# A two-attention, two-mixture kernel: norms and routing of five batches moved to other steps, exponentials cut into other pieces, causal copies of 384 and 320 columns

## The reference, cut to what matters

```
x = x + attn_a(layernorm(x))   # 16 heads of 64, relative bias, softmax over all 256 keys
x = x + ffn(layernorm(x))      # 8 experts, one per row (argmax of a router), gated
x = x + attn_b(layernorm(x))   # keys and values through a 128-wide latent, CAUSAL softmax
x = x + ffn(layernorm(x))      # the same experts again
```

```
scores = q @ k.T * scale (+ bias, or -inf above the diagonal)
attn   = softmax(scores, axis=-1)
out    = attn @ v ; heads joined ; @ w_out
```

## Time and profile before

| | |
|---|---|
| median of three runs | 674.76 us |
| lowest, highest | 671.71, 675.14 us |
| the profiled execution | 671.86 us |
| its span, first to last instruction | 670.6 us |
| TensorE busy | 637.2 us, 95% |
| ScalarE busy | 543.8 us, 81% |
| VectorE busy | 512.4 us, 76% |
| GpSimd busy | 354.6 us, 53% |

### The profile page before, as it was taken

How to read it: one execution, slowest core, us unless ns; L and a number is a source line. 1 busy time by engine, 2 the same in 40 slices (tenths; PEclk the granted TensorE clock), 3 DMA queues, 4 the chain that set the end, 5 groups by cost and what they waited for, 6 DMA issues and landing times. The chain is left out here.

```text
span 670.6 us, 22111 instructions
## 1 busy us (share of the span) xinstructions
PE 637.2 (95%) x7454; PEld 536.2 (80%) x7454; DVE 512.4 (76%) x2211; ACT 543.8 (81%) x1776; POOL 354.6 (53%) x669
## 2 busy tenths in 40 slices
PE   5899999999999999989999999999999999999997
PEld 5578787777778787879996788878788878878987
DVE  4977878987887878988656767787878777888833
ACT  3898888889898979775765999898989898986664
POOL 4454545566445744732116545464757574572746
PEclk9999999999999999999999999999999999999999
DMA  8999989999980000035521000000000000013140
GB/s 270 276 312 304 277 212 326 305 306 304 284 258 10 26 2 2 34 97 140 148 67 40 22 3 1 3 2 11 17 14 10 14 26 2 3 34 96 55 131 17
DMA packets 90319, 74.78 MB, mean 112 GB/s; under 512 B 12225, under 2 KB 87111, under 8 KB 90080
## 3 DMA queue, kind: packets, MB, share of 16 engines
q1 hardware_dynamic: 86512, 66.24, 35.0%
q0 software_dynamic: 2848, 6.33, 2.9%
q10 hardware_dynamic: 848, 0.79, 0.4%
HBM read 19.93 MB, written 54.00 MB: 110 GB/s over the span
## 5 line engine op out<-in xcount | busy, mean ns | idle before, releaser
L392 POOL TENSOR_SCALAR ring<-ring,rs 128x256 f32<-128x256 f32 (+1 forms) x500 | 218.3, 455 | 205.2 <-DVE rs L1310 204.8
L990 ACT ACTIVATE ring<-ring,mn 128x256 f32<-128x256 f32 (+1 forms) x512 | 242.0, 479 | 2.9 <-DVE mn L1298 2.8
L531 PE MATMUL ps<-ident,ring 128*128 128x128 f32 x896 | 124.9, 275 | 4.0 <-DVE ol L1270 2.9
L644 PE MATMUL ps<-qk 64*64 64x256 f32 (+1 forms) x2048 | 112.4, 356 | 1.4 <-DVE mn L1298 0.7
L531 PEld LDWEIGHTS ps<-ident,ring 128*128 128x128 f32 x896 | 101.6, 143 | 14.8 <-issue 7.3
L687 PE MATMUL ps<-pt,v 64*64 64x256 f32 (+3 forms) x2048 | 103.1, 339 | 6.4 <-ACT pt L977 5.6
L687 PEld LDWEIGHTS ps<-pt,v 64*64 64x64 f32 x2048 | 73.8, 133 | 37.6 <-ACT pt L977 18.6
L990 ACT ACTIVATION_READ_ACCUMULATOR ring<-ring,mn 128x1 f32 x512 | 99.9, 195 | 0.0
L1325 DVE COPY pt<-ps 128x512 f32<-128x512 f32 (+1 forms) x128 | 71.3, 557 | 32.7 <-PE ps L531 31.3
L962 ACT COPY qk<-ps 128x512 f32<-128x512 f32 x128 | 74.4, 581 | 21.3 <-PE ps L528 20.3
L644 PEld LDWEIGHTS ps<-qk 64*64 64x64 f32 x2048 | 65.8, 132 | 29.9 <-issue 12.4
(11 more groups left out here) (209 smaller groups left out, 1300.2 us busy)
## 6 DMA issues: line engine op xcount, KB each, us to landing
xs_scratch<-f_ys SPq DMA_DIRECT2D x16, 2064.0 KB, 22.0
yr_scratch<-f_ys SPq DMA_DIRECT2D x8, 1024.0 KB, 10.1
f_xs<-xs_scratch SPq DMA_DIRECT2D x50, 129.0 KB, 2.5
w<-in_W SPq DMA_DIRECT2D x16, 256.0 KB, 5.9
xs_scratch<-f_ys SPq DMA_DIRECT2D x2, 1677.0 KB, 20.9
yr_scratch<-f_ys SPq DMA_DIRECT2D x25, 64.0 KB, 1.8
T<-in_bias SPq DMA_DIRECT2D x2, 512.0 KB, 7.8
T<-in_bias SPq DMA_DIRECT2D x1, 1024.0 KB, 10.3
```

Of the source, the lines that this page charges most:

```text
L392: i = pool.tensor_scalar(part, part, rs[:, q], 1.0, ALU.mult, ALU.mult)
L531: return pe.transpose(out, src, ident[:, :])
L644: i = pe.matmul(PS[u % 2][hh][cols, 256 * it:256 * it + w], qk[rows, 128 * it + 64 * half_:128 * it + 64 * half_ + 64], qk[rows, 256:256 + ...
L990: i = act.activation(part, part, ACT.Exp, bias=mn[:, q], scale=-1.0, accum_out=sm[:, q])
```

## The change

Five things change, in the tables of lags and in the functions that read them.

1. For batches 0 to 4 (`CALM` = 5) the norms after the attention, the choice and the places move to other steps, given by `CALM_POST`, and VectorE does them in a new function `calm(s)`, called in even steps directly behind its copy of transposes `TR(s-4)`. Before, they stood before that copy, behind it in odd steps, or at the end of an odd step. The places are cut into two parts, two steps apart. TensorE's, ScalarE's and GpSimd's shares follow.
2. For batches 2 to 7 the norm before the attention moves one step earlier (`CALM_PRE`) and also into `calm(s)`.
3. The exponentials of an even unit are taken as piece (0,0) at the start of the next even step but before the copy `T(s)`, pieces (0,1) and (1,0) after the copy of transposes, and piece (1,1) in the odd step. Before, it was two pieces in the even step and two in the odd.
4. In the causal attention the transposes are spread over the two banks as 3 and 3 in place of 4 and 2. ScalarE copies 384 columns in place of 512, VectorE 320 columns in one run in place of 2 x 128.
5. The fetches of the last four x tiles in stage 1 (`FETCH`) move from steps 35, 39, 41, 43 to 18, 26, 32, 34.

The diff, cut to its core:

```diff
-POST = {"a": 14, "b": 15, "c": 16, "lg": 16, "gate": 17, "d": 18, "place": 18}
+POST = {"sums": 13, "pow": 13, "a": 14, "xn": 14, "b": 15, "c": 16, "lg": 16, "choose": 16, "gate": 17, "d": 18, "place": 18}
+CALM = 5
+CALM_POST = {"sums": 14, "pow": 14, "a": 20, "xn": 20, "b": 22, "c": 23, "lg": 23, "choose": 26, "gate": 27, "d": 28, "counted": 28, "place": 30}
+CALM_PRE = {"a": -8, "pow": -8, "a2": -6}
...
-FETCH = dict(zip((35, 39, 41, 43), range(*CH[1])))
+FETCH = dict(zip((18, 26, 32, 34), range(*CH[1])))
...
+    def keys_at(q, causal):
+
+        return ((0, 0), (1, 0), (1, 128), (0, 128))[q] if causal else (q // 2, 256 * (q % 2))
...
-            act.copy(pt[:, 0, :], PP[0][:, :]).then_inc(a_pt0, 1)
+            w = 384 if causal else 512
+            act.copy(pt[:, 0, 0:w], PP[0][:, 0:w]).then_inc(a_pt0, 1)
...
+            if s % 2 == 0 and 2 <= s < NU:
+                expo(s - 2, ALL[0])
             if 0 <= s < NU:
                 T(s)
...
-                expo(s - 3, (1,))
+                expo(s - 3, *ALL[3:])
...
-                expo(s - 2, (0, 1) if s % 2 or s == NU else (0,))
+                expo(s - 2, *(ALL if s % 2 or s == NU else ALL[1:3]))
...
-            late = slice(128 if causal else 0, 256)
-            dve.tensor_copy(*(a.rearrange("p (q i) -> p q i", q=2)[:, :, late] for a in (pt[:, 1, :], PP[1][:, :]))
-                            ).then_inc(v_pt1, 1)
+            r = slice(64, 384) if causal else slice(0, 512)
+            dve.tensor_copy(pt[:, 1, r], PP[1][:, r]).then_inc(v_pt1, 1)
...
+            calm(s)
             if s < NU and (b := post_at(s, "a")) is not None:
                 post_a2(b)
...
+        def calm(s):
+            if (b := calm_pre(s, "a")) is not None:
+                pre_a(b)
+            if (b := calm_pre(s, "a2")) is not None:
+                pre_a2(b)
+            if (b := calm_post(s, "sums")) is not None:
+                sums(b)
+            if (b := calm_post(s, "a")) is not None:
+                post_a(b)
+                post_a2(b)
+            if (b := calm_post(s, "choose")) in ROUTED:
+                decide(b)
+            if (b := calm_post(s, "counted")) in ROUTED:
+                place(*ROUTED[b], NR * st + ROUTE_NO[b], (0,))
+            if (b := calm_post(s, "place")) in ROUTED:
+                place(*ROUTED[b], NR * st + ROUTE_NO[b], (1,))
```

More of the change, by code:

```diff
@@ L103, in pre_at @@
     b = at(s, PRE[part])
-    return None if not b or (st and b == 1 and part in PRE_1) else b
+    return None if not b or (st and b == 1 and part in PRE_1) or (b >= 2 and part in CALM_PRE) else b
 def post_at(s, part):
@@ L111, in post_at, with calm_post, calm_pre, either @@
     b = at(s, POST[part])
-    return b if b is not None and b < NB - 1 else None
+    return b if b is not None and CALM <= b < NB - 1 else None
+def calm_post(s, part):
+    b = at(s, CALM_POST[part])
+    return b if b is not None and b < CALM else None
+def calm_pre(s, part):
+    b = at(s, CALM_PRE[part])
+    return b if b is not None and b >= 2 else None
+def either(s, part):
+    return [b for b in (calm_post(s, part), post_at(s, part)) if b is not None]
 def nrm1_by_dve(u):
@@ L450, in step @@
                     send()
-            if (b := post_at(s, "place")) is not None and b in ROUTED:
-                to_send.extend((j, ROUTE_NO[b], b) for j in range(*ROUTED[b]))
+            for b in either(s, "place"):
+                to_send.extend((j, ROUTE_NO[b], b) for j in range(*ROUTED.get(b, (0, 0))))
                 while to_send and b >= NB - 2:
@@ L891, in after @@
         def after(s):
-            if (b := post_at(s, "b")) is not None and b < NB - 2:
-                post_b(b)
-            if (b := post_at(s, "c")) is not None:
+            for b in either(s, "b"):
+                if b < NB - 2:
+                    post_b(b)
+            for b in either(s, "c"):
                 post_c(b)
-            if (b := post_at(s, "d")) is not None and b in ROUTED:
-                post_d(b)
+            for b in either(s, "d"):
+                if b in ROUTED:
+                    post_d(b)
             if st == 0:
@@ L1129, in after @@
         def after(s):
[L1130 to L1135, removed]
+            for b in either(s, "b"):
+                if b < NB - 1:
+                    post_b(b)
+            for b in either(s, "gate"):
+                if b in ROUTED:
+                    gates(b)
+            for b in either(s, "d"):
+                if b in ROUTED:
+                    post_d(b)
             if st == 0:
@@ L1552, in step @@
                 index(3)
-            if (b := at(s, 13)) is not None and b < NB - 1:
+            if s < NU and (b := post_at(s, "sums")) is not None:
                 sums(b)
@@ L1608, in routes @@
                 post_c(b)
+            if (b := post_at(s, "choose")) is not None and b in ROUTED:
+                decide(b)
             if (b := post_at(s, "place")) is not None and b in ROUTED:
```

89 lines of the change are left out of this document (47 added, 42 removed).

## The result

The changed kernel took 655.33 us in the median of four runs (653.98 to 655.89), the kernel before 673.82 us in the median of its four. The ratio is 0.9726, with a 95% interval from 0.9693 to 0.9758. Run a second time, beside other kernels, it was 0.9755 (0.9742 to 0.9769). So it is 2.4 to 2.7% faster, 16.5 to 18.5 us, where I forecast 663 us, a gain of 10.3 us or 1.5%, and a range that ended at 656. The direction and the places were right; the gain is more than half as large again as the sum of 10.3 us.

The account below looks back on a forecast made before the run. TensorE was taken to wait for `pt`, `ph` and a PSUM bank, with ScalarE nearly full. Second attention 5.8 + 2.5 + 1.2 - 1.0 = 8.5 us, first 1.8, together 10.3: 663 us, range 656 to 671.

Parts of the forecast that it names:

- a tie of ScalarE with TensorE: Second attention: ScalarE's pair 6.35 us after the change, TensorE's 6.24; so 5.8 of 7.6 and 2.5 of 3.2 taken.
- double blocks: Two moved VectorE blocks in one even step exceed the room: 1.0 us lost in second attention, 0.3 in first.
- the bank wait of the second attention: TensorE's transposes wait for the PSUM bank that `ol` frees, behind VectorE's statistics; moving these gains 1.2 us.
- PV behind `pt`: Second attention: PV starts late, held by ScalarE's `pt` copy, 7.6 us over 30 pairs; 5.8 us to be gained.
- The two factors: Odd step: one exponential fewer before `pt`, about 0.4 us earlier; copies of about 475 (ScalarE) and 490 ns (VectorE).
- 2.5 for `ph`: Second attention: TensorE's wait for `ph` before its transposes goes in five batches, 3.2 us, of which 2.5 taken.
- The first attention: Gain of 1.8 us: 0.8 for `ph`, 0.6 for the bank, 0.7 for PV in routed pairs, less 0.3.
- the middle that I took: 663 us, between 661.6 from the profiled execution of 671.86 and 664.5 from the median of 674.76.
- TensorE was not full: Rival that TensorE is full and the gaps are an artefact of modelled matmul ends: 672 to 674 us, chance 0.08.
- ScalarE did not take over: Rival that ScalarE becomes the limit of the second attention, so only its shortening counts: 668 us, chance 0.20.
- VectorE was not late: Rival that moved blocks delay VectorE's odd `pt` copy and PV, making the kernel slower: 679 us, chance 0.10.
- The signs that I had named: PV 1.35 to 1.45 us after scores, `ph` waits only in batches 5 and 6, `pt` copies near 475 and 490 ns.

Follow-up runs that it names:

- N alone: Norms, choice, places and fetches moved on the kernel before, with the old exponential pieces and old causal copies: ratio 0.9918 of the time before.
- E alone: The exponentials' new pieces on the kernel before, with nothing else changed: ratio 0.9913 of the time before.

## Why the prediction was wrong

The mechanism was the one forecast; the sizes of its terms were not. By the two stretches 16.0 us were gained where the sum had 10.3. Of the 5.7 us between, 2.2 were taken off for a tie of ScalarE with TensorE that cost nothing, 2.2 are the waits of the first attention, 0.75 are double blocks that cost less, and 0.6 is the bank wait of the second attention.

**PV behind `pt`.** I saw the right wait, in the right 16 pairs, and its cause (they were not always the third and fourth pair of a batch, as I wrote: the second pair of the first and of the last batch had it too). I took 5.8 of 7.6 us; 7.3 went. The two factors were right in size: the stretch from `qk` to `pt` fell by 0.38 us, the copies took 476 and 489 ns for my 475 and 490. The even `qk` did not become late. Of the 1.8 us that I took off for ScalarE's tie with TensorE, 1.5 were not due: ScalarE is full in the middle pairs and still on time.

**Norms in the second attention.** The terms were 2.5 for `ph`, 1.2 for the bank and 1.0 against for double blocks, net 2.7. The second attention gained 12.0 us, so 4.7 beside the 7.3. The 0.7 us taken off `ph` for the same tie was not due: TensorE's wait behind `ph` fell by 3.3 us. The bank was worth 1.8 and not 1.2, by the kernel that puts the statistics back. The double blocks cost 0.25 us, not 1.0: only two pairs, with PV at 1.48 and 1.47 us, show one. The experiments say why: the room is 1.6 to 1.7 us, and blocks that I had put at 1.7 to 1.8 nearly fit, while 3.0 do not.

**The first attention** is the step that failed most for its size: 1.8 us forecast, 4.0 gained. The step was "TensorE lost about 0.2 us there in eight even steps of the second and four of the first", with 0.17 for `ph`. I had found the lost time by comparing each group of matmuls with the shortest of its kind, and where every batch lost the same in the same place, the shortest had it too. The lengths of whole pairs show it. Before, the pairs from 65.57 us on took

```profile
65.57:73.81 8.24, 8.09 (x98) 6.28 (x97) 7.88 (x33) 7.14 (x24) 4.74 (x10) 1.00 1.09 313
73.81:81.89 8.08, 8.08 (x100) 6.51 (x99) 6.02 (x24) 7.07 (x23) 5.00 (x10) 1.00 1.07 288
81.89:89.89 8.00, 7.98 (x96) 6.00 (x95) 6.75 (x28) 7.48 (x25) 4.35 (x9) 1.00 0.46 56
```

and after

```profile
72.44:80.11 7.67, 7.67 (x97) 6.06 (x96) 6.68 (x30) 7.04 (x24) 4.71 (x9) 1.00 0.99 277
80.11:87.84 7.73, 7.73 (x97) 6.07 (x96) 6.45 (x26) 7.05 (x24) 4.41 (x9) 1.00 0.46 56
...
98.78:107.05 8.27, 8.27 (x102) 6.66 (x101) 6.80 (x30) 7.02 (x24) 3.85 (x9) 1.00 1.11 331
```

The pair of 8.27 now holds `ph` and the router product (0.37 us), which had been in the next pair. So the first pair lost 8.24 + 0.37 - 8.27 = 0.34 us, twice the 0.17 that `ph` showed, and the third 8.00 - 7.73 = 0.27. That is 0.6 us a batch, where the sum had 0.17 for `ph` and 0.6 us for the banks of the whole attention, about 0.3 a batch. The experiments bear it out: N alone gave 3.1 us there, and putting back only the norm before the attention cost 1.0, where I had put the banks at 0.6. E alone gave 1.2, half of it before PV and half in the pairs with statistics; the sum had a share of 0.7 us for it.

**The base.** By spans the change is 16.4 us, by the first median 18.5, by the second 16.5. In later runs the kernel before had medians of 672.5 and 672.8, so that the 674.76 it showed first was some 2 us high, and the middle that I took was a little high as well; it is a small part of the miss.

**The rivals.** TensorE was not full: the two stretches became 16 us shorter at unchanged weight loads. ScalarE did not take over in the full change, but it does in the kernel with N alone (PV excess 9.3), so the case was real and the 0.2 us of the copies with the 0.4 of the pieces decided it. VectorE was not late in the full change. It was in two other kernels, in single pairs: with whole places, and with only the norm before the attention moved. The latter gained 3.0 us in all; its `pt` copy was late in four pairs as this rival has it, and beside that the router's addition stood behind the moved block, which I had not named.

**The uncertainty.** The range ended at 656 with "all bounds good". The bounds as written give 7.6, 3.2, 2.4, 0.8 and 0.7, in sum 14.7 us, so 657.2 from the lower base, and the stretches alone gained 16.0. Two terms of the first attention had no bounds at all (0.8 for `ph`, 0.7 for the routed pairs), and the bank waits, with 2.4 us at most, measured 2.8.

**The new profile.** The signs that I had named came out but for the batches: those of the second attention take 28.7 to 29.8 us where I had said 30, and those of the first 34.0 to 35.0 where I had said 35.0.

## What to carry to other kernels

When engines wait for each other around a loop, take the excess of whole periods over the shortest possible one, not of single groups over their own minimum, and count all of it for a change that clears all of the waits. Judge such parts together: here three of them alone shortened the second attention by 4.4, 1.9 and 3.1 us and together by 12.0, and of the two halves of one of them one alone cost 3.4 us and gave 2.8 beside the other. Measure the room between two deadlines before filling it, and look for what else stands behind the block, a small addition that frees a bank as much as the large copy.

## What the runs showed of the hardware

An indirect DMA occupies GpSimd for 1.05 us as the first and 0.96 as the second of two, with 0.17 and 0.30 us of issue in front (alike within 0.01 us in six pairs of sends), so two together are 2.5 us in which it multiplies nothing. And in the second attention the wide exponentials took 510 ns in the mean after, against 501 before, the narrow ones 402 against 403; what lengthened the wide ones was not tried.
